# Sorting five of eight batches by expert in a cross-attention and mixture-of-experts kernel

## The chip, the cores and the metric

The kernel runs on one core of a Trainium2 chip. The metric is the device time of one launch in microseconds (us), as the median over runs.

## The reference

The input x is 8 batches of 128 tokens with 256 features, ctx_512 is 8 x 128 x 64. One layer of cross attention (16 heads of 16 features, causal) and one mixture of experts follow each other. The second part is what the change touches:

```python
x = x + xattn(layernorm(x), ctx_512, ...)
xf = layernorm(x)                                    # 1024 tokens x 256
router_logits = xf @ gate_weight.T + xf @ gate_delta.T       # 8 experts
probs = softmax(router_logits)
routing_weights, selected = top_k(probs, 2)
routing_weights = routing_weights / routing_weights.sum(-1, keepdims=True)
gup = einsum('th,eho->teo', xf, gate_up_proj) + lora part    # 256 -> 2 x 128, for every expert
gates, h = split(gup, 2, axis=-1)
h = silu(gates) * h
out = einsum('tei,eih->teh', h, down_proj) + lora part       # 128 -> 256
y = einsum('tkh,tk->th', take_along_axis(out, selected), routing_weights)
x = x + y
```

Each token uses two of the eight experts. The lora parts are folded into the weights once, ahead of the tokens.

## The kernel before

A batch is a tile of 128 tokens. The attention stage goes over the batches one after the other (`for b in range(NT)` on each engine), with scores of batch b + 2, exponentials of b and output projection of b - 2 interleaved. As each batch leaves it, its residual is added, it is normalised (`second_stats` on DVE, `normaliser` on POOL, `x2_normalise` on ACT), transposed (`x2_T` on PE) and split in a high and a low fp32r part (`x2T_high`, `x2T_low`), so that three fast fp32r matmuls stand for one in full precision. The weights are split the same way, `merge_high` on ACT and `merge_lows` on POOL.

The expert stage is dense: every token goes through all eight experts, and a weight that is zero for the six experts not chosen takes them out. Tokens form two groups (NG = 2) of four batches, 512 tokens (GN). The router of a group is `router_logits`, `lg_T`, `route_logits`, `route_choose`, `route_weights`, `w_T`. The weights, transposed to one row per expert, are stored to memory (`w_dram`, L218) and read back as a broadcast to 128 partitions, one 256 KB load for each expert (L226), into `weight_all`, which shares the tile `probsT` with attention. Then 16 steps n follow, 8 experts for each group. A step is on PE `gate_step` and `up_step` (six matmuls each, 512 moving columns, weights stationary, all recorded as L798) and `down_step` (12 matmuls with 256 moving columns, L1087), which sums all experts of a group in two banks; on ACT `silu_step` and `h_high`; on DVE `gate`, `weigh` and `h_low` (L664, L671, L676). PE runs gate_step four steps and up_step three steps ahead of down_step. At a group's end DVE adds the banks to `x_sb` (`add_residual`, L654) and SP stores the result (L231). The order on every engine is written out by hand; semaphores tie them together. In `link` a DVE or POOL instruction is waited for by the next one of its engine.

## Time and profile before

| | |
|---|---|
| median of 3 runs | 170.81 us (170.69 to 171.04) |
| the profiled execution | 170.58 us, its span 168.8 us |
| busy | PE 153.3, DVE 105.4, ACT 80.1, POOL 53.5 us |
| instructions | 3777 |
| granted clock of TensorE, mean | 0.998 |

The span runs from the first to the last instruction; what lies around it is not in the profile. Busy time of an engine is a share of the whole span. PE is matmuls, PEld the loads of their stationary operand, which lie beside matmuls.

### The profile page before, as it was taken

Reading aid. Unit: us, or ns where it says so; the run is one execution under the profiler, and the core shown is the slowest. Engines: PE = TensorE matmul, PEld = TensorE weight load, DVE = VectorE, ACT = ScalarE, POOL = GpSimd, SP = SyncE. Lnnn points to the kernel's source line nnn. Section 1 sums busy time; section 2 is a strip of 40 time slices with the busy share of each in tenths; the row PEclk is TensorE's granted clock in tenths of the full one; section 3 lists DMA queues with packets and bytes.
Section 4 is the critical chain, followed back from the end, with each engine's and each line's share of the span. In section 5 each row is a group of like instructions: output and inputs, shape, how many; then the busy total and the mean of one; then the engine's idle time right before and its main releaser. Section 6 shows DMA issues by size and latency. Waiting matters only on the chain.

```text
span 168.8 us, 3777 instructions
## 1 busy us (share of the span) xinstructions
PE 153.3 (91%) x1481; PEld 118.9 (70%) x1481; DVE 105.4 (62%) x224; ACT 80.1 (47%) x161; POOL 53.5 (32%) x93
## 2 busy tenths in 40 slices
PE   0597999999999999999999997999969989999972
PEld 0365676677777677778778876887758868888961
DVE  2778986859657657835498456555943466444463
ACT  1373557356657776586754617422653022222420
POOL 4276002256378657776740243330000000000000
PEclk9999999999999999999999999999999999999999
DMA  5999940000000000000000185000000594000003
GB/s 148 292 255 229 282 126 2 6 6 0 8 0 8 0 6 2 4 2 4 0 0 4 37 257 209 0 4 0 2 0 4 144 344 137 0 0 0 4 0 124
DMA packets 13042, 11.18 MB, mean 66 GB/s; under 512 B 6457, under 2 KB 10449, under 8 KB 13025
## 3 DMA queue, kind: packets, MB, share of 16 engines
q1 hardware_dynamic: 9584, 7.14, 15.7%
q0 software_dynamic: 544, 2.10, 4.6%
q10 hardware_dynamic: 2896, 1.70, 3.9%
q8 instruction: 12, 0.20, 0.5%
q14 instruction: 6, 0.04, 0.1%
HBM read 9.79 MB, written 1.08 MB: 64 GB/s over the span
## 4 chain that ended last, share of the span: by engine, by line
PE 65%; DVE 14%; DMA 8%; ACT 5%; issue 5%; POOL 1%; DVEq 0%; ACTq 0%
PE bank L798 29%; PE bank L1087 9%; PE bank L908 8%; DMA probsT<-weights 4%; PE bank L894 4%; PE bank L1024 4%; PE bank L915 3%; DVE m_sb L593 2%; DVE h_f L671 2%; DMA x_sb<-in_x 2%; DMA weights<-wT 2%; DVE xhat L552 2%; PE bank L973 2%; ACT silu L410 1%; DVE stats L539 1%
## 5 line engine op out<-in xcount | busy, mean ns | idle before, releaser
L798 PE MATMUL bank<-xT_hi,up_hi 128*128 128x512 f32 x64 | 27.1, 424 | 3.0 <-ACT silu L410 3.0
L318 ACT ACTIVATE h_hi<-h_f 128x512 fp32r<-128x512 f32 x16 | 10.1, 632 | 37.2 <-PE bank L1087 25.9
L295 POOL TENSOR_SCALAR_AFFINE_SELECT probsT<-probsT 128x512 f32<-128x512 f32 x32 | 19.7, 635 | 22.5 <-ACT probsT L391 22.5
L593 DVE TENSOR_REDUCE m_sb<-bank 128x4 f32<-128x512 f32 x32 | 20.4, 685 | 9.4 <-PE bank L908 9.4
L391 ACT ACTIVATE probsT<-bank 128x512 f32<-128x512 f32 x32 | 17.9, 590 | 17.3 <-PE bank L915 17.3
L798 PE MATMUL bank<-xT_hi,up_lo 128*128 128x512 f32 x64 | 25.3, 395 | 0.0
L798 PE MATMUL bank<-xT_lo,up_hi 128*128 128x512 f32 x64 | 25.3, 395 | 0.0
L676 DVE TENSOR_TENSOR h_lo<-h_f,h_hi 128x512 fp32r<-128x512 f32 x16 | 11.4, 713 | 21.0 <-ACT h_hi L318 21.0
L1087 PE MATMUL bank<-dn_hi,h_hi 128*128 128x256 f32 x64 | 18.4, 288 | 1.1 <-DVE h_lo L676 1.0
L915 PE MATMUL bank<-q_f,k_f 32*128 32x128 f32 x256 | 18.6, 283 | 0.0
L798 PEld LDWEIGHTS bank<-xT_hi,up_hi 128*128 128x128 f32 x64 | 12.0, 188 | 8.6 <-ACT silu L410 6.9
L1087 PE MATMUL bank<-dn_hi,h_lo 128*128 128x256 f32 x64 | 17.9, 279 | 0.0
L1087 PE MATMUL bank<-dn_lo,h_hi 128*128 128x256 f32 x64 | 17.8, 279 | 0.0
L908 PEld LDWEIGHTS bank<-k_f,q_f 32*128 32x128 f32 x256 | 13.6, 186 | 5.5 <-issue 5.0
L908 PE MATMUL bank<-k_f,q_f 32*128 32x128 f32 x256 | 16.3, 283 | 0.0
L915 PEld LDWEIGHTS bank<-q_f,k_f 32*128 32x128 f32 x256 | 15.5, 186 | 0.7 <-issue 0.7
L671 DVE TENSOR_TENSOR h_f<-probsT,gated 128x512 f32<-128x512 f32 x16 | 12.0, 748 | 5.1 <-DMA probsT<-weights 4.7
L798 PEld LDWEIGHTS bank<-xT_hi,up_lo 128*128 128x128 f32 x64 | 12.0, 188 | 2.9
L1087 PEld LDWEIGHTS bank<-dn_hi,h_hi 128*128 128x128 f32 x64 | 12.0, 187 | 2.1 <-DVE h_lo L676 1.5
L286 POOL TENSOR_TENSOR up_lo<-up_w,up_hi 128x512 fp32r<-128x512 f32 x8 | 10.3, 1291 | 9.8 <-ACT up_hi L318 9.8
L798 PEld LDWEIGHTS bank<-xT_lo,up_hi 128*128 128x128 f32 x64 | 12.1, 188 | 1.7
L1087 PEld LDWEIGHTS bank<-dn_lo,h_hi 128*128 128x128 f32 x64 | 12.0, 188 | 0.4
(137 smaller groups left out, 284.4 us busy)
## 6 DMA issues: line engine op xcount, KB each, us to landing
probsT<-weights SPq DMA_DIRECT2D x16, 256.0 KB, 5.5
x_sb<-in_x SPq DMA_DIRECT2D x4, 256.0 KB, 4.8
up_w<-in_L_ffn_gate_up_proj ACTq DMA_DIRECT2D x1, 1024.0 KB, 10.4
up_w<-in_L_ffn_gate_up_proj POOLq DMA_DIRECT2D x1, 1024.0 KB, 7.2
dn_w<-in_L_ffn_down_proj POOLq DMA_DIRECT2D x1, 1024.0 KB, 9.3
out<-x_sb SPq DMA_DIRECT2D x4, 256.0 KB, 2.2
ctx_sb<-in_ctx ACTq DMA_DIRECT2D x2, 128.0 KB, 5.6
wq_raw<-in_L_xattn_Wq ACTq DMA_DIRECT2D x1, 256.0 KB, 5.8
```

What stands on the lines that cost most here:

```text
L286: pool.tensor_tensor(merge_slice(up_lo, dn_lo, n), merge_slice(up_w, dn_w, n), merge_slice(up_hi, dn_hi, n).bitcast(F32), ALU.subtract).th ...
L295: pool.affine_select(out=ch, in_=ch, compare_op=ALU.is_ge, fill=0.0, base=0, pattern=[[0, 4], [1, P]], channel_multiplier=-1).then_inc(S_( ...
L318: act.activation(out_, in_, ACT.Copy, scale=scale).then_inc(S_(done), 1)
L391: act.activation(probsT[:, b % 2, 4 * j:4 * j + 4, :].rearrange("p h n -> p (h n)"), bank[2 + j % 2][:, :], ACT.Exp).then_inc(S_("exp_done ...
L593: dve.reduce_max(m_sb[:, b % 2, :].rearrange("p (u j t) -> p j u t", u=2, t=2)[:, c], S_BANK(b, c)[:, :].rearrange("p (u t n) -> p u t n", ...
L671: dve.tensor_tensor(h_f[:, k, :], weight_all[:, n % E, :], gated[:, k, :], ALU.mult).then_inc(S_("h_ready"), 1)
L676: dve.tensor_tensor(h_lo[:, k, :], h_f[:, k, :], h_hi[:, k, :].bitcast(F32), ALU.subtract)\
L798: last = pe.matmul(out_, a, m, start=start and i == 0, stop=stop and i == len(pairs) - 1, **kw)
L894: pe.matmul(S_BANK(s, j)[:, :], ident_b[:, :], causal[:, :, :].rearrange("p h n -> p (h n)"), start=True, stop=True, skip_group_check=True)
L908: last = pe.matmul(S_BANK(s, j)[:, c * P:(c + 1) * P], q_f[rows, c, tokens(s)], k_f[rows, c, tokens(s)], start=False, stop=True, skip_grou ...
L915: last = pe.matmul(bank[2 + j % 2][:, c * P:(c + 1) * P], k_f[rows, c, tokens(t)], q_f[rows, c, tokens(t)], start=True, stop=True)
L1087: last = pe.matmul(bank[6 + t // 2][:, (t % 2) * H:(t % 2 + 1) * H], a[:, k, tok], w[:, e, :], start=i == 0 and t % 2 == 0 and m == 0, sto ...
```

## The change

Batches 0 to 2 (384 tokens, DN) go through the dense stage as before, now in 8 steps. The weights of its router are computed inside the attention loop's last step, and Silu's table is loaded ahead by one activation (`warm`). Batches 3 to 7 (640 tokens) are sorted by expert:

- `choose`, `positions` and `slots` find for each token its two experts and its two row numbers in a buffer `xs` in memory, which has 640 rows for each expert. Ones below the diagonal (`tri`) times the choice counts the tokens ahead within a batch, `ahead` carries the count over batches. This is done for batches 3 and 4, then 5 and 6, then 7.
- POOL scatters every normalised row twice (`scatter_rows`, 10 indirect transfers); a row of 272 elements also carries the number of the row in `ys` where its result belongs. ACT fills xs with a blank before (`fill`).
- `map_tiles` works out which expert and which row of xs each of 17 tiles of 128 rows has. 17 is the most that 1280 rows in 8 groups can need.
- SP reads the row number of each tile into a register and loads the tile. PE reads the weights' column into a register (`pick`) and uses it in nine matmuls: `gate_up_tile` has the tokens stationary and 256 columns of weights moving, `hidden_T` transposes the hidden part, `down_tile` has 256 moving columns.
- POOL scatters the 128 rows of a tile's result into `ys` (`scatter_tile`). When all have landed, SP loads five blocks back (`yg`), DVE (batches 3, 5, 7) and ACT with POOL (4, 6) weigh and add the two rows of each token, and five stores follow.

On DVE the routing stands inside the dense steps: `choose(2)` at n = 0, `choose(3)` and `slots(2)` at n = 1, `slots(3)` and `map_tiles` at n = 2; `choose(1)` and `slots(1)` stand ahead of the loop. ACT and DVE go through the tiles with `silu_tile(n + 1)`, `hT_high(n)`, `x_copy(n + 3)`, `y_copy(n - 1)` and `gate_tile(n + 1)`, `hT_low(n)`, `x_low(n + 3)`, `row_of_y(n)`. `pair_weights` and its Exp come after the last tile. The core of the diff:

```diff
+    DENSE = range(0, 3)
+    SORTED = range(3, NT)
+    DN = len(DENSE) * P
+    NS = len(SORTED)
+    ROWS = NS * P
+    TILES = (2 * ROWS + E * (P - 1)) // P
+    XW = 272
+    BY_DVE = (3, 5, 7)
+    BY_POOL = (4, 6)
+    ROUTED = (tuple(DENSE), (3, 4), (5, 6), (7,))
...
+        xs = nc.dram_tensor("xs", (E * ROWS + P, XW), F32, kind="Internal").ap()
+        ys = nc.dram_tensor("ys", (TILES * P + 2 * ROWS, H), F32, kind="Internal").ap()
+        w_dram = nc.dram_tensor("weights", (E, DN), F32, kind="Internal").ap()
...
+        load_of = lambda n: (0, 1, 1, 2, 2, 2, 3, 3, 3, 3, 4, 4, 4, 4, 5, 5, 5)[n]
...
-            for g in range(NG):
-                sp.wait_ge(S_("wT_copied"), g + 1)
-                sp.dma_start(w_dram[g], wT[:, g, :]).then_inc(S_("w_written"), 16)
-                sp.wait_ge(S_("w_written"), 16 * (g + 1))
-                for i in range(E):
-                    if g == 0:
-                        sp.wait_ge(S_("pv_done"), NT - 1 if i < E // 2 else NT)
-                    else:
-                        sp.wait_ge(S_("h_ready"), i + 1)
-                    e = EXPERTS[i]
-                    sp.dma_start(weight_all[:, i, :], w_dram[g, e:e + 1, :].to_broadcast([P, GN])).then_inc(weight_loaded[i], 16)
...
+            sp.wait_ge(S_("wT_copied"), 1)
+            sp.dma_start(w_dram, wT[:, :]).then_inc(S_("w_written"), 16)
+            sp.wait_ge(S_("w_written"), 16)
+            for i in range(E):
+                sp.wait_ge(S_("pv_done"), NT - 1 if (i + 1) * DN <= NH * P else NT)
+                e = EXPERTS[i]
+                sp.dma_start(weight_all[:, i, :], w_dram[e:e + 1, :].to_broadcast([P, DN])).then_inc(weight_loaded[i // 2], 16)
+            sp.wait_ge(S_("tiles_mapped"), 1)
+            sp.wait_ge(S_("x_scattered"), 16 * 2 * NS)
+            for n in range(TILES):
+                row = sp.value_load(row_x[0:1, n:n + 1], min_val=0, max_val=E * ROWS)
+                sp.dma_start(xt[:, n, :], xs[bass.ds(row, P), :]).then_inc(tile_loaded[load_of(n)], 16)
...
+            sp.wait_ge(S_("y_scattered"), 16 * TILES)
+            for j, b in enumerate(SORTED):
+                sp.dma_start(yg[:, :, j, :], ys[TILES * P:, :].rearrange("(k j p) c -> j p k c", k=2, p=P)[j])\
+                    .then_inc(y_back[(j + 1) // 2], 16)
+            for n, b in enumerate(BY_DVE):
+                sp.wait_ge(S_("pair_added"), n + 1)
+                sp.dma_start(out_v[:, b, :], x_sb[:, b, :]).then_inc(S_("stored"), 16)
+            sp.wait_ge(S_("stored"), 16 * (2 + NS))
...
+            def scatter_rows(t):
+                j = t - SORTED[0]
+                pool.wait_ge(S_("slots_ready"), [t in r for r in ROUTED].index(True))
+                if j == 0:
+                    pool.wait_ge(S_("filled"), 16 * 3)
+                for k, name in enumerate(("x2row_ready", "x2row_again")):
+                    pool.wait_ge(S_(name), j + 1)
+                    pool.indirect_dma_start(xs, bass.IndirectOffsetOnAxis(ap=index[:, k, t:t + 1], axis=0), xrow[:, j, k, :], None,
+                                            bounds_check=E * ROWS - 1).then_inc(S_("x_scattered"), 16)
+            def scatter_tile(n):
+                pool.wait_ge(S_("y_copied"), n + 1)
+                pool.wait_ge(S_("y_row_ready"), n + 1)
+                pool.indirect_dma_start(ys, bass.IndirectOffsetOnAxis(ap=y_row[:, n:n + 1], axis=0), y_at(n),
+                                        None, bounds_check=TILES * P + 2 * ROWS - 1).then_inc(S_("y_scattered"), 16)
...
-            for t in range(NT - 3, NT):
-                normaliser(1, t, t + 1, "mv2_ready", t + 1)
-            merge_lows(4)
+            normaliser(1, 5, 6, "mv2_ready", 6)
+            normaliser(1, 6, 7, "mv2_ready", 7)
+            scatter_rows(3)
+            normaliser(1, 7, 8, "mv2_ready", 8)
+            scatter_rows(4)
+            merge_lows(2)
+            scatter_rows(5)
+            scatter_rows(6)
+            merge_lows(1)
+            scatter_rows(7)
+            merge_lows(1)
+            for n in range(TILES):
+                scatter_tile(n)
+            for n, b in enumerate(BY_POOL):
+                j = b - SORTED[0]
+                for k in range(2):
+                    pool.wait_ge(S_("y_weighed"), 2 * n + k + 1)
+                    ins = pool.tensor_tensor(x_sb[:, b, :], yg[:, k, j, :], x_sb[:, b, :], ALU.add)
+                    if k == 0:
+                        link(ins)
+                    else:
+                        ins.then_inc(S_("pool_added"), 1)
...
+            def fill(lo, hi):
+                act.wait_ge(S_("blank_made"), 1)
+                rows = xs[lo * P:hi * P, :].rearrange("(r p) c -> p r c", p=P)
+                act.dma_start(rows, blank[:, None, :].to_broadcast([P, hi - lo, XW])).then_inc(S_("filled"), 16)
...
+            def x_copy(n):
+                act.wait_ge(S_("xt_T"), n + 1)
...
+                copy(xh_hi[:, n % 3, :, :], XT_BANK(n), "xt_copied")
+            def silu_tile(n):
+                act.wait_ge(S_("gu_ready"), n + 1)
...
+                act.activation(silu_t[:, n % 2, :], bank[2 + n % 2][:, 0:I], ACT.Silu).then_inc(S_("silu_tile"), 1)
+            def hT_high(n):
+                act.wait_ge(S_("hT_ready"), n + 1)
...
+                copy(hT_hi[:, n % 2, :], bank[n % 2][:, 0:P], "hT_high")
+            def y_copy(n):
+                act.wait_ge(S_("tile_down"), n + 1)
+                copy(y_at(n), bank[6 + n % 2][:, 0:H], "y_copied")
...
+            def choose(r):
+                ts = ROUTED[r]
...
+                other = lg[:, lo:hi, None, :].to_broadcast([P, n, E, E])
+                own = lg[:, lo:hi, :, None].to_broadcast([P, n, E, E])
+                fork(dve.tensor_tensor(outranks[:, 0:n, :, 0:E], other, own, ALU.is_gt))
+                link(dve.tensor_tensor(outranks[:, 0:n, :, E:2 * E], other, own, ALU.is_equal))
+                link(dve.tensor_tensor(outranks[:, 0:n, :, E:2 * E], outranks[:, 0:n, :, E:2 * E],
+                                       earlier[:, None, :, :].to_broadcast([P, n, E, E]), ALU.mult))
+                join()
+                link(dve.reduce_sum(rank[:, lo:hi, :], outranks[:, 0:n, :, :], AX.X))
+                link(dve.tensor_scalar(chosen[:, lo:hi, :], rank[:, lo:hi, :], 1.5, None, ALU.is_lt))
...
+            def slots(r):
+                ts = ROUTED[r]
+                lo, hi = ts[0], ts[-1] + 1
...
+                link(dve.tensor_tensor(slot[:, lo:hi, :], slot_at(r, lo, hi).rearrange("p (t e) -> p t e", e=E),
+                                       chosen[:, lo:hi, :], ALU.mult))
+                fork(dve.reduce_max(both[:, 0, lo:hi], slot[:, lo:hi, :], AX.X))
+                link(dve.reduce_sum(slot_sum[:, lo:hi], slot[:, lo:hi, :], AX.X))
+                join()
+                link(dve.tensor_tensor(both[:, 1, lo:hi], slot_sum[:, lo:hi], both[:, 0, lo:hi], ALU.subtract))
+                dve.tensor_scalar(index[:, :, lo:hi], both[:, :, lo:hi], -1.0, None, ALU.add).then_inc(S_("slots_ready"), 1)
+            def map_tiles():
+                n = TILES
+                dve.wait_ge(S_("pos_ready"), len(ROUTED) - 1)
+                link(dve.tensor_tensor(over[:, :, :], count_at[:, :, None].to_broadcast([1, E, NS]), full[:, :, :], ALU.is_gt))
+                link(dve.reduce_sum(n_tiles[:, :], over[:, :, :], AX.X))
+                fork(dve.tensor_scalar(skip[:, :], n_tiles[:, :], -float(P), float(ROWS), ALU.mult, ALU.add))
...
+                link(dve.tensor_scalar(w_at[:, :], n_done[:, :], E - 1.0, float(H), ALU.min, ALU.mult))
+                dve.tensor_scalar(row_x[:, :], row_f[:, :], float(E * ROWS), None, ALU.min).then_inc(S_("tiles_mapped"), 1)
...
+            def x_low(n):
+                dve.wait_ge(S_("xt_copied"), n + 1)
...
+                dve.tensor_tensor(xh_lo[:, n % 3, :, :], XT_BANK(n), xh_hi[:, n % 3, :, :].bitcast(F32), ALU.subtract)\
+                    .then_inc(S_("x_low"), 1)
+            def gate_tile(n):
+                dve.wait_ge(S_("silu_tile"), n + 1)
...
+                dve.tensor_tensor(ht_f[:, n % 2, :], bank[2 + n % 2][:, I:2 * I], silu_t[:, n % 2, :], ALU.mult)\
+                    .then_inc(S_("gated_tile"), 1)
+            def hT_low(n):
+                dve.wait_ge(S_("hT_high"), n + 1)
...
+                dve.tensor_tensor(hT_lo[:, n % 2, :], bank[n % 2][:, 0:P], hT_hi[:, n % 2, :].bitcast(F32), ALU.subtract)\
+                    .then_inc(S_("hT_copied"), 1)
+            def row_of_y(n):
+                dve.wait_ge(tile_loaded[load_of(n)], 16 * loaded_with[n])
+                dve.tensor_tensor(y_row[:, n:n + 1], xt[:, n, H:H + 1].bitcast(I32), dump[:, n:n + 1], ALU.max)\
+                    .then_inc(S_("y_row_ready"), 1)
...
+            def positions(r):
+                pe.wait_ge(S_("chosen_ready"), r)
+                for t in ROUTED[r]:
+                    j = t - SORTED[0]
+                    products(slot_at(r, t, t + 1), [(tri[:, :], chosen[:, t, :]), (ones[:, :], ahead[:, j, :])],
+                             "pos_ready" if t == ROUTED[r][-1] and t != NT - 1 else None)
+                    if t == NT - 1:
+                        products(count_at, [(ones[:, 0:1], ahead[:, j + 1, :])], "pos_ready")
...
+            def tile_T(n):
+                pe.wait_ge(tile_loaded[load_of(n)], 16 * loaded_with[n])
+                if n == 0:
+                    pe.wait_ge(S_("slots_ready"), 2)
+                elif n == 1:
+                    pe.wait_ge(S_("tiles_mapped"), 1)
+                else:
+                    pe.wait_ge(S_("x_low"), n - 1)
+                for ic in range(HC):
+                    last = pe.transpose(XT_BANK(n)[:, ic, :], xt[:, n, ic * P:(ic + 1) * P], ident[:, :])
+                last.then_inc(S_("xt_T"), 1)
+            def pick(n):
+                if n == 0:
+                    pe.wait_ge(S_("tiles_mapped"), 1)
+                columns[n] = pe.value_load(w_at[0:1, n:n + 1], min_val=0, max_val=(E - 1) * H)
+            def gate_up_tile(n):
+                if n < 2:
+                    pe.wait_ge(S_("gated_ready"), E - 1 + n)
+                else:
+                    pe.wait_ge(S_("gated_tile"), n - 1)
+                pe.wait_ge(S_("x_low"), n + 1)
+                picked = lambda w, ic: w[:, ic, :, :].rearrange("p e o -> p (e o)")[:, bass.ds(columns[n], 2 * I)]
+                products(bank[2 + n % 2][:, 0:2 * I],
+                         [(a[:, n % 3, ic, :], picked(w, ic)) for ic in range(HC)
+                          for a, w in ((xh_hi, up_hi), (xh_hi, up_lo), (xh_lo, up_hi))], "gu_ready")
+            def hidden_T(n):
+                pe.wait_ge(S_("gated_tile"), n + 1)
+                if n < 2:
+                    pe.wait_ge(S_("silu_ready"), E - 1 + n)
+                else:
+                    pe.wait_ge(S_("hT_copied"), n - 1)
+                pe.transpose(bank[n % 2][:, 0:P], ht_f[:, n % 2, :], ident[:, :]).then_inc(S_("hT_ready"), 1)
+            def down_tile(n):
+                pe.wait_ge(S_("hT_copied"), n + 1)
+                if n < 2:
+                    pe.wait_ge(S_("out_ready"), n + 1)
+                else:
+                    pe.wait_ge(S_("y_copied"), n - 1)
+                picked = lambda w: w[:, :, :].rearrange("p e h -> p (e h)")[:, bass.ds(columns[n], H)]
+                products(bank[6 + n % 2][:, 0:H], [(a[:, n % 2, :], picked(w)) for a, w in
+                                                   ((hT_hi, dn_hi), (hT_hi, dn_lo), (hT_lo, dn_hi))], "tile_down")
...
-            for n in range(NG * E):
-                if n + 3 < NG * E:
+            for n in range(E):
+                if n + 3 < E:
                     up_step(n + 3)
-                if n + 4 < NG * E:
+                if n == 0:
+                    x2_T(NT - 1)
+                    logits(2)
+                if n == 1:
+                    positions(2)
+                if n + 4 < E:
                     gate_step(n + 4)
-                if n in (0, 1):
-                    x2_T(NT - 2 + n)
+                if n == 0:
+                    logits(3)
                 if n == 2:
-                    router_logits(1, bank[5])
-                if n == 3:
-                    lg_T(1, bank[5])
-                if n == 5:
-                    w_T(1, bank[5])
+                    positions(3)
+                if n >= E - 2:
+                    tile_T(n - (E - 2))
                 down_step(n)
+            for n in range(3):
+                pick(n)
+            gate_up_tile(0)
+            tile_T(2)
+            for n in range(TILES):
+                if n + 1 < TILES:
+                    gate_up_tile(n + 1)
+                if n + 3 < TILES:
+                    tile_T(n + 3)
+                hidden_T(n)
+                if n:
+                    down_tile(n - 1)
+                if n + 3 < TILES:
+                    pick(n + 3)
+            down_tile(TILES - 1)
```

## Rows read from the trace of the kernel before

**Rows 1.** The page: busy time by engine.

```profile
PE 153.3 (91%) x1481; PEld 118.9 (70%) x1481; DVE 105.4 (62%) x224; ACT 80.1 (47%) x161; POOL 53.5 (32%) x93
```

**Rows 2.** Windows: length, busy us of PE, PEld, DVE, ACT, POOL, clock, DMA, GB/s.

```profile
0.00:83.60 83.60, 75.52 (x1022) 55.17 (x1023) 56.78 (x131) 49.60 (x108) 43.27 (x79) 1.00 0.31 70
83.60:101.20 17.60, 17.60 (x115) 14.11 (x113) 12.10 (x33) 7.94 (x15) 6.25 (x12) 1.00 0.22 69
101.20:136.30 35.10, 32.12 (x179) 25.76 (x178) 19.69 (x37) 15.23 (x26) 4.01 (x3) 1.00 0.19 57
136.30:158.20 21.90, 21.88 (x122) 18.32 (x123) 11.50 (x19) 5.59 (x10) 0.00 (x0) 1.00 0.21 73
158.20:168.80 10.60, 6.16 (x48) 5.54 (x47) 5.37 (x9) 1.75 (x3) 0.00 (x0) 0.97 0.15 49
...
20.00:30.00 10.00, 9.85 (x130) 7.01 (x131) 7.70 (x15) 6.26 (x14) 1.22 (x2) 1.00 0.32 90
```

**Rows 3.** Chain of waits: start, duration, what.

```profile
86.64 0.22 PE bank L1005 x2
...
93.88 1.44 DMA weights<-wT
...
95.34 3.55 DMA probsT<-weights
...
142.33 1.41 PE bank L1087 x12
143.74 2.93 PE bank L798 x12
```

**Rows 4.** Timeline of the end of the span: start, duration, engine.

```profile
165.21 0.28 PE L1087 MATMUL bank<-dn_hi,h_lo 128*128 128x256 f32 x1
165.54 1.07 SPq L231 DMA_DIRECT2D out<-x_sb  x2
```

**Rows 5.** Timeline of DVE, 85 to 97 us.

```profile
85.90 0.39 DVE L633 TENSOR_TENSOR above<-lg 128x256 f32<-128x256 f32 x1
86.33 0.43 DVE L634 TENSOR_TENSOR equal<-lg 128x256 f32<-128x256 f32 x1
...
88.72 0.18 DVE L644 TENSOR_TENSOR lpick<-lexp,chosen 128x32 f32<-128x32 f32 x1
88.94 0.19 DVE L645 TENSOR_REDUCE lsum<-lpick 128x4 f32<-128x32 f32 x1
...
95.54 0.42 DVE L615 TENSOR_TENSOR x_sb<-bank,x_sb 128x256 f32<-128x256 f32 x1 [1.81 <-PE bank L798]
```

**Rows 6.** Groups of DVE: operation, shapes, count, busy us, mean ns, idle before.

```profile
L664 DVE TENSOR_TENSOR gated<-bank,silu 128x512 f32<-128x512 f32 x16 | 10.9, 684 | 1.3 <-ACT silu L410 1.3
...
L535 DVE SCALAR_TENSOR_TENSOR xT_lo<-bank,xT_hi 128x256 fp32r<-128x256 f32 x8 | 3.4, 424 | 2.9 <-ACT xT_hi L318 2.8
```

**Rows 7.** Groups of instructions of ACT.

```profile
L318 ACT ACTIVATE o_T<-bank 128x256 f32<-128x256 f32 x8 | 3.0, 380 | 3.4 <-PE bank L984 3.4
...
L410 ACT ACT_TABLE_LOAD x2 | 2.6, 1283 | 0.0
...
L318 ACT ACTIVATE mT<-bank 16x128 f32<-16x128 f32 x8 | 2.0, 251 | 0.8 <-PE bank L938 0.8
```

**Rows 8.** Groups of instructions of POOL.

```profile
L286 POOL TENSOR_TENSOR up_lo<-up_w,up_hi 128x512 fp32r<-128x512 f32 x8 | 10.3, 1291 | 9.8 <-ACT up_hi L318 9.8
...
L270 POOL DMA_DIRECT2D up_w<-in_L_ffn_gate_up_proj x1 | 1.1, 1110 | 0.0
L273 POOL DMA_DIRECT2D dn_w<-in_L_ffn_down_proj x1 | 0.9, 932 | 0.0
```

**Rows 9.** Timeline of SP's queue, 93 to 103 us.

```profile
95.34 4.38 SPq L226 DMA_DIRECT2D probsT<-weights  x8
```

**Rows 10.** Issues of DMA: count, KB each, median us to landing.

```profile
probsT<-weights SPq DMA_DIRECT2D x16, 256.0 KB, 5.5
...
out<-x_sb SPq DMA_DIRECT2D x4, 256.0 KB, 2.2
```

564 lines of the change are left out of this document (370 added, 194 removed).

## The prediction, made before the kernel ran

> **What bounds the kernel now.** I read the page first. PE is busy for 91% of the span, far ahead of DVE, ACT and POOL [rows 1]. Next the table of windows: the attention stage ends near 83.6 us, and from there to the last matmul PE leaves little open (17.60 of 17.60, 32.12 of 35.10, 21.88 of 21.90 us), at the full clock of 2.4 GHz (1.00) [rows 2]. So the second half is a queue of matmuls, and only fewer matmul columns can shorten it much. The chain of waits then gives the unit of that half: one expert step of a group of 512 tokens takes 2.93 us for 12 matmuls of gate and up and 1.41 us for 12 of down, 4.34 us together, and there are 16 such steps, 69.4 us [rows 3]. The same chain shows where PE waited: the routing weights go out to memory (1.44 us) and come back to all partitions (3.55 us) [rows 3], and the same once more for the second group, near 130 us. Last, the end: the last matmul runs from 165.21 to 165.49 us, and an addition and a store follow, 3.3 us to the end of the span [rows 4].
>
> **The change part by part, on PE.** A matmul over 512 moving columns costs 2.93/12 = 0.244 us, one over 256 costs 1.41/12 = 0.118 us [rows 3]. Halfway between them, 384 columns are 0.181 us. The dense stage with three batches: 12 x 0.181 + 9 x 0.118 = 3.23 us a step, 8 steps 25.8 us. A sorted tile has the tokens stationary and 256 weight columns moving: 6 x 0.118 + 3 x 0.118 = 1.06 us. Its three transposes cost 0.11 us each, since a pair takes 0.22 [rows 3]: 0.33 us. That is 1.39 us a tile and 23.6 us for 17. Expert work on PE falls from 69.4 to 49.4 us: 20.0 us taken off the engine that sets the end. The sorting is paid for by latency: routing before, a trip through memory before, and one behind.
>
> **When the dense stage ends.** The first expert matmul stays near 83.6 us. In the window 83.60:101.20 before, PE did nine half steps (9 x 1.47 = 13.2 us), which leaves 4.4 us for other things (values, output projections, transposes) [rows 2]; I count 6 us for these with the small matmuls of logits, positions and later transposes. PE alone would end the dense stage at 83.6 + 6 + 25.8 = 115.4 us. But DVE has to route in the middle of it. A small DVE instruction with its link to the next costs 0.22 us, a larger one 0.45 us [rows 5]. From these, choosing for batches 5 and 6 is about 2.2 us, for batch 7 1.6, two times slots 2.2, the map of tiles (13 instructions) 2.9: 8.9 us, all within the first three expert steps. Gate, weigh and low part of a step are 3 x 0.57 = 1.7 us at 384 columns (0.69 at 512, 0.42 at 256) [rows 5, 6]. So these three steps take DVE 3 x 1.7 + 8.9 = 14.0 us where PE needs 9.7, and each down step waits for its low part. DVE enters them near 96 us, as the last batch's residual was added at 95.54 [rows 5], and leaves them at 110. Behind that lie three half steps (3 x 1.09), five down steps (5 x 1.06), two transposes of tiles (0.4) and some 1.5 us of waits on gate and low part: 120.5 us, 5 us behind what PE alone could do. Two things come back: the weights of the dense batches are chosen while attention still runs, so the first trip (93.88 to 98.89 us) starts about 7 us earlier, as soon as values(7) frees its tile, and the second trip, with the switch to Exp and back (1.28 us each) [rows 7], is gone. Both are in the sum, as it counts no bubbles of their kind.
>
> **When the first tile can start.** Slots of batch 7 are ready near 108.5 us by that count. POOL has then two scatters of 5, two of 6, a merge of 1.29 us [rows 8] and two of 7. No indirect scatter is in this trace; nearest is POOL's own issue of a plain DMA, 0.93 to 1.11 us [rows 8]. The price may be as low as the 0.55 us of an issue on SP or as high as the 2.2 us in which a store lands [rows 9, 10]; I take 1.1, because it is the same engine. Then all rows are in memory near 116 us, and tile 0, with one load behind it, is there at about 118.5 us. Tiles 1 and 2 follow by 121. I put the first sorted matmul at 122.5 us, 2 us behind the dense stage: three picks in a row stand in front of it on PE, and only one down step can lie over them. I add 1.0 us for the group of tiles 3 to 5: SP issues one load in 0.55 us (eight in 4.38) [rows 9] and must also read a row number first, so 17 loads take some 20 us, slower at the start than the tiles are wanted.
>
> **The loop of 17 tiles.** ACT has two operations of 128 columns (0.25 us each, after mT) and two of 256 (0.38 each) [rows 7]: 1.26 us. DVE has 0.42 + 2 x 0.30 + 0.18 = 1.20 us [rows 5, 6]. POOL has one scatter, 1.1 us. SP has about 1.2 us. All are under PE's 1.39, and every tile is buffered at least twice, so no handoff closes a circle within a tile. What the trace cannot price is the register: one read on PE's queue for each tile (pick) and nine matmuls whose weights it names. Bounds: nothing, since PE's queue runs ahead while matmuls are pending; 0.55 us, the nearest instruction that a sequencer handles by itself, when nothing hides it. pick stands behind down_tile(n - 1), whose three matmuls (0.35 us) lie over it, and what is queued behind it is the next gate_up_tile, for which ACT and DVE then wait. I take 0.16 us exposed, 1.55 us a tile: 26.4 us. The two ends are 23.6 and 33.0 us.
>
> The Trainium skill (DMA: Bandwidth & Descriptors, section Latency and other measured facts) puts a floor of about 600 ns under a tensor_load, the read of a register. No run here shows one yet. By that rule, an estimate with all of it exposed, a tile would take 1.99 us and the whole would be 171.8 us.
>
> **The tail.** Behind the last down matmul: copy of y 0.4; its scatter on POOL 1.1; landing in memory 2.2, as a store to out; five loads issued on SP at 0.55, 2.7; the last one lands 3.0 later (the first broadcast took 3.55, the median of sixteen queued ones was 5.5) [rows 3, 9, 10]; two additions 0.8; store 2.2: 12.4 us, against 3.3 before [rows 4]. The pair weights and the load of Exp's table (1.28 us, about 3 us together) lie beside the scatter and the loads. Bounds: 9 us if issues and landings overlap, 17 us if the loads take the 5.5 us and the scatter 2.2.
>
> **Other edits** cost nothing that shows. The added constants on POOL, some twenty operations of 0.1 to 0.5 us, come behind the load of dn_w, beside a POOL that is busy 1.22 us of the ten from 20 to 30 us [rows 2]; if they delay the first mask they cost up to 3 us. The fill of the 41 blocks of xs on ACT's queue is three issues of 0.55 us [rows 9] in the attention stage, where ACT is busy 49.60 of 83.60 us [rows 2].
>
> **The sum.** 122.5 + 1.0 + 26.4 + 12.4 = 162.3 us of span against 168.8. The profiled execution took 170.58 us, 1.8 us outside its span, and the median of the runs is 0.2 above it: 164.3 us, 3.8% faster than 170.81.
>
> **Rivals.** *PE's queue becomes the bound.* The register read and the nine matmuls with a computed address take more of PE's queue than the matmuls hide. For it: nine of twelve matmuls of a tile are affected, and the wait in front of down_tile leaves the queue little lead: the high and low copies of a tile's hidden part come 0.25 + 0.30 us and some 0.2 of handoffs behind its transpose, the down step one tile time (1.39) behind it, so about 0.6 us. Against it: matmul pairs go out every 0.118 us now with nothing visible between them. It decides from 0.38 us more a tile (6.5/17), at 1.93 us; 0.55 us exposed gives 170.9, and with 0.03 us more for each of the nine matmuls, 2.2 us a tile, 175.4 us, slower. *The scatters on POOL set the loop.* At 2.2 us each the loop takes 37 us and the scatters of x another 4 us late: 179 us; at 1.6 us it is hardly seen. For it, only that this trace has no scatter. *The sorted stage starts late.* Routing, scatter and loads are one chain through five engines; if first tiles come 6 us later, PE idles, the clock may be taken down (0.97 in the last window, where PE was busy 6.16 of 10.6 us [rows 2]), and the time is 170 us, no change. *Everything overlaps.* DVE catches up, the first sorted matmul is at 118.5 us, a tile takes 1.40 us and the tail 10 us: 118.5 + 0.5 + 23.8 + 10 + 2 = 154.8 us.
>
> **Chances.** The forecast, with a tile at 1.4 to 1.85 us and the stage ends 3 us to either side: 0.52, own range 158 to 170. Everything overlaps 0.10. Late start 0.13, split evenly about no change (0.05, 0.03, 0.05). PE's queue 0.18, nearly all slower (0.01 no change). Scatters 0.07. Faster 0.52 + 0.10 + 0.05 = 0.67, within 0.2% (about what a measurement of this kernel can tell from no change) 0.04, slower 0.29. The range runs from the overlapping case to the slow queue, 156 to 175 us; beyond lie half of the overlapping case, most of the scatters and the worst of the queue.
>
> **What the profile after would show.** Dense gate matmuls at 0.18 us, the first tile matmul near 122.5 us, tiles every 1.55 us, the last down matmul near 150 us, then 12 us of copy, scatter, load and store. In the chain of waits the loop should be PE's. If it shows issue on PE between down_tile and gate_up_tile, the queue is the bound; if y_scattered comes long after the last copy, POOL is. A hole on PE ahead of the first tile means that routing is late. Most likely wrong are the price of a register-named tile and the 5 us that PE loses to routing on DVE.

## The result and the profile after

The changed kernel takes 183.37 us, median of 4 runs (181.49 to 187.41), beside 170.93 (170.69 to 171.39) for the kernel before on the same chip: a ratio of 1.061, 95% interval 1.056 to 1.066. It is slower by 6.1%; 164.3 us were predicted. Ratios here and below rest on the executions within 1.5% of the kernel's fastest, and two of these four lie above that, with a lower clock (185.09 and 187.41 us). Its profiled execution took 181.49 us, its span 179.7 us, where the sum of the prediction gave 162.3.

The page's first row, to be held against [rows 1]:

```profile
PE 143.6 (80%) x1493; PEld 116.1 (65%) x1493; DVE 115.8 (64%) x311; ACT 90.0 (50%) x220; POOL 86.5 (48%) x141
```

The 20 us of matmuls that the change takes away are not to be seen: busy PE fell from 153.3 to 143.6 us. The windows say why, and where the time is (attention stage, then the stretch to the first sorted tile, the tiles, the tail; columns as in [rows 2]):

```profile
0.00:83.60 83.60, 75.95 (x1025) 55.85 (x1026) 57.16 (x132) 48.65 (x107) 45.77 (x95) 1.00 0.47 138
83.60:101.20 17.60, 15.49 (x124) 13.83 (x122) 12.36 (x38) 9.38 (x21) 7.05 (x13) 1.00 0.34 105
101.20:131.40 30.20, 24.33 (x145) 22.07 (x145) 24.40 (x60) 10.13 (x22) 13.71 (x14) 0.89 0.19 63
131.40:163.20 31.80, 27.86 (x200) 24.38 (x200) 17.52 (x70) 18.20 (x66) 14.38 (x15) 1.00 0.40 124
163.20:179.70 16.50, 0.00 (x0) 0.00 (x0) 4.42 (x12) 3.66 (x7) 5.61 (x7) 0.58 0.44 144
```

From 101.2 to 131.4 us DVE and PE are busy alike (24.4 and 24.3 us of 30.2), neither of them full, and the mean clock is 0.89: it stands at 1.2 GHz from 104.5 to 107.9 and from 121.6 to 125.0 us. The last dense matmul ends at 130.50 us, where the prediction had 120.5, and the first sorted one comes at 131.46 us, 9 us behind the 122.5 of the prediction.

The chain of waits through the start of that stage and its third and fourth tiles (start, duration, what):

```profile
127.00 1.96 DMA xt<-xs
129.00 0.44 PE bank L1426 x2
129.44 1.06 PE bank L1408 x9
130.50 0.96 issue
131.46 0.97 PE bank L1096 x6
...
135.84 0.97 PE bank L1096 x6
136.81 0.22 PE bank L1426 x2
137.03 0.11 PE bank L1451
137.13 0.35 PE bank L1096 x3
137.49 0.18 issue
137.67 1.02 PE bank L1096 x6
```

First PE waits for a tile from memory, then 0.96 us for nothing that the profile shows; those are the three picks. From there a tile takes 1.82 to 1.96 us, but for one of 2.22 (135.84 to 137.67 is 1.83), of which 1.39 are matmuls and transposes as priced. The reads of a register on PE's queue, from the view of that line (minimum/median/maximum ns, first and last start):

```profile
L1432 PEldq TENSOR_LOAD <-w_at x17: 297/302/706, 129.1 to 157.7; - x17
L1432 PEldq FUSED_REGOPS  x17: 146/151/165, 129.6 to 158.1; - x17
L1432 PEldq SEQ_ASSERT  x17: 18/18/28, 129.8 to 158.3; - x17
```

Four rows of DVE's timeline and four of POOL's in the dense stage:

```profile
104.58 2.76 DVE L838 TENSOR_TENSOR outranks<-lg 128x128 f32<-128x128 f32 x1
107.26 0.28 DVE L839 TENSOR_TENSOR outranks<-lg 128x128 f32<-128x128 f32 x1
...
117.67 1.99 DVE L893 TENSOR_SCALAR row_x<-row_f 1x17 int32<-1x17 f32 x1
...
121.77 2.25 DVE L970 TENSOR_TENSOR h_lo<-h_f,h_hi 128x384 fp32r<-128x384 f32 x1 [0.59 <-ACT h_hi L449]
```
```profile
104.67 1.28 POOL L382 TENSOR_TENSOR dn_lo<-dn_w,dn_hi 128x512 fp32r<-128x512 f32 x1
105.90 1.27 POOL L382 TENSOR_TENSOR up_lo<-up_w,up_hi 128x512 fp32r<-128x512 f32 x1
...
118.34 1.28 POOL L382 TENSOR_TENSOR dn_lo<-dn_w,dn_hi 128x512 fp32r<-128x512 f32 x1
...
122.31 1.29 POOL L382 TENSOR_TENSOR dn_lo<-dn_w,dn_hi 128x512 fp32r<-128x512 f32 x1
```

An instruction of 0.28 us took 2.76, one of 0.17 took 1.99, one of 0.56 took 2.25: 6.0 us more, and each ends within 0.5 us of the end of POOL's additions. By the profile `row_x`, begun at 117.67 us, is late before the addition begins at 118.34, while an indirect scatter still runs on POOL; e4 decides between the two.

The tail, in the chain of waits:

```profile
163.78 0.98 POOL ys L399
164.76 0.30 issue
165.06 2.42 DMA ys<-xt,y_row
...
168.43 4.32 DMA probsT<-ys
...
172.83 0.52 ACT probsT L712
...
173.42 1.01 POOL x_sb L439
...
174.50 0.61 POOL x_sb L439
...
175.25 0.90 POOL x_sb L439
```

The last down matmul ends at 163.11 us and the span at 179.7: 16.6 us, for which 12.4 were predicted. POOL starts the last scatter 1.5 us after its data are there, a load lands after 4.32 us, and two batches are added on POOL.

### The profile page after: what moved, and what is told of

The parts are those of the page before. It is cut to its first block, busy times and chain, and to the rows that moved or that the text cites. A ratio compares the mean times of both kernels' runs of the same rounds, so it can differ in the third digit from the quotient of the medians.

```text
span 179.7 us, 4442 instructions
## 1 busy us (share of the span) xinstructions
PE 143.6 (80%) x1493; PEld 116.1 (65%) x1493; DVE 115.8 (64%) x311; ACT 90.0 (50%) x220; POOL 86.5 (48%) x141
## 3 DMA queue, kind: packets, MB, share of 16 engines
q10 hardware_dynamic: 8480, 7.68, 13.3%
## 4 chain that ended last, share of the span: by engine, by line
PE 49%; DVE 16%; issue 11%; POOL 9%; DMA 8%; ACT 2%; SPq 2%; POOLq 1%; DVEq 0%; ACTq 0%
PE bank L1096 22%; PE bank L1206 7%; PE bank L1192 4%; POOL xs L393 3%; PE bank L1332 3%; PE bank L1213 3%; DMA probsT<-ys 2%; DVE m_sb L795 2%; PE bank L1426 2%; POOL ys L399 2%; DMA x_sb<-in_x 2%; DVE outranks L838 2%; DVE xhat L754 2%; POOL x_sb L439 1%; DMA xs<-xrow,index 1%
## 5 line engine op out<-in xcount | busy, mean ns | idle before, releaser
L399 POOL DMA_INDIRECT ys<-xt,y_row x17 | 16.6, 977 | 25.8 <-DVE y_row L948 24.4
L1206 PE MATMUL bank<-k_f,q_f 32*128 32x128 f32 x256 | 16.3, 283 | 0.0
L393 POOL DMA_INDIRECT xs<-xrow,index x10 | 10.4, 1039 | 10.0 <-DVE index L874 7.5
L1096 PE MATMUL bank<-up_hi,xh_hi 128*128 x34 | 11.2, 328 | 4.3 <-DVE ht_f L936 2.2
L1096 PE MATMUL bank<-xT_hi,up_hi 128*128 128x384 f32 x32 | 12.2, 380 | 2.0 <-DVE gated L958 2.0
L578 ACT ACTIVATE silu_t<-bank 128x128 f32<-128x128 f32 x17 | 4.7, 278 | 13.5 <-PE bank L1096 12.2
L1096 PE MATMUL bank<-xT_hi,up_lo 128*128 128x384 f32 x32 | 11.1, 348 | 0.0
L1096 PEld LDWEIGHTS bank<-up_hi,xh_hi 128*128 128x128 f32 x34 | 6.4, 187 | 7.3 <-issue 7.3
L1096 PE MATMUL bank<-xT_lo,up_hi 128*128 128x384 f32 x32 | 10.9, 341 | 0.0
L1192 PE MATMUL bank<-causal,ident_b 128*128 128x512 bf16 x32 | 9.6, 380 | 1.2 <-DVE q_f L766 0.5
L1096 PE MATMUL bank<-up_lo,xh_hi 128*128 x34 | 9.6, 284 | 0.0
L1096 PE MATMUL bank<-up_hi,xh_lo 128*128 x34 | 9.5, 280 | 0.0
```

Source lines behind the costliest of these rows:

```text
L393: pool.indirect_dma_start(xs, bass.IndirectOffsetOnAxis(ap=index[:, k, t:t + 1], axis=0), xrow[:, j, k, :], None, bounds_check=E * ROWS - ...
L399: pool.indirect_dma_start(ys, bass.IndirectOffsetOnAxis(ap=y_row[:, n:n + 1], axis=0), y_at(n), None, bounds_check=TILES * P + 2 * ROWS - ...
L1096: last = pe.matmul(out_, a, m, start=start and i == 0, stop=stop and i == len(pairs) - 1, **kw)
L1192: pe.matmul(S_BANK(s, j)[:, :], ident_b[:, :], causal[:, :, :].rearrange("p h n -> p (h n)"), start=True, stop=True, skip_group_check=True)
L1206: last = pe.matmul(S_BANK(s, j)[:, c * P:(c + 1) * P], q_f[rows, c, tokens(s)], k_f[rows, c, tokens(s)], start=False, stop=True, skip_grou ...
```

## The experiments

Each profile is cut at the same three points: the first dense matmul (86.05 us in the changed kernel), the first tile matmul, the start of the last down matmul. "Low" is the time at 1.2 GHz before the tail, and behind it how much of that lies between the first dense and the first tile matmul. All in us; the median has the fastest execution beside it. The kernel before had medians of 170.8 to 171.4 us beside them.

| kernel | median (fastest) | first dense | to first tile | tiles | tail | low (in "to first tile") |
|---|---|---|---|---|---|---|
| prediction | 164.3 | 83.6 | 38.9 | 27.4 | 12.4 | 0 |
| changed | 183.37 (181.49) | 86.05 | 45.4 | 31.4 | 16.9 | 6.8 (6.8) |
| e1 | 184.62 (182.83) | 87.80 | 46.6 | 31.7 | 17.8 | 17.1 (12.5) |
| e2 | 182.84 (180.75) | 89.21 | 45.5 | 30.3 | 17.3 | 14.3 (6.8) |
| e3 | 182.59 (180.84) | 86.24 | 45.2 | 31.6 | 16.6 | 3.4 (3.4) |
| e4 | 183.25 (181.44) | 88.36 | 44.9 | 31.5 | 16.6 | 13.7 (6.8) |
| e5 | 183.27 (182.24) | 90.23 | 49.8 | 26.0 | 16.3 | 23.9 (12.2) |
| e6 | 183.69 (182.31) | 90.92 | 46.5 | 32.4 | 14.6 | 23.9 (8.9) |
| e7 | 180.01 (176.66) | 88.84 | 41.0 | 31.5 | 16.2 | 10.2 (4.0) |
| e8 | 179.03 (174.58) | 90.61 | 46.8 | 25.9 | 14.7 | 23.9 (12.6) |
| e9 | 175.72 (173.94) | 88.42 | 39.4 | 31.3 | 14.9 | 6.8 (3.4) |
| e10 | 174.02 (173.44) | 86.30 | 39.4 | 31.5 | 15.0 | 6.8 (3.4) |
| e11 | 174.59 (173.49) | 85.93 | 40.3 | 31.3 | 14.8 | 6.8 (6.8) |
| e12 | 173.88 (173.32) | 86.23 | 39.3 | 31.5 | 15.0 | 3.4 (3.4) |
| e13 | 170.97 (170.37) | 86.64 | 39.3 | 28.1 | 14.9 | 3.4 (3.4) |
| e14 | 168.20 (167.57) | 86.25 | 40.6 | 24.9 | 15.1 | 6.8 (6.8) |
| e15 | 168.26 (167.78) | 86.06 | 40.5 | 24.8 | 15.1 | 6.8 (6.8) |
| e16 | 178.14 (177.63) | 90.34 | 45.7 | 25.5 | 16.7 | 17.1 (8.6) |

The clock falls for 3.4 or 6.8 us at a time; the expectations below, read from coarser windows, say 3.5 and 7.5. What 3.4 us more of it cost can be read from e11, e14 and e15 beside e9, e12 and e13: 0.9 to 1.2 us to the first tile (e14 and e15 also differ in their reads).

**e1: the pick earlier in the tile.**

```diff
                 if n + 1 < TILES:
                     gate_up_tile(n + 1)
                 if n + 3 < TILES:
+                    pick(n + 3)
                     tile_T(n + 3)
...
-                if n + 3 < TILES:
-                    pick(n + 3)
```

> PE's pick of tile n+3 stands directly behind gate_up_tile(n+1), ahead of tile_T(n+3), instead of behind down_tile(n-1). The loop of the changed kernel takes 1.83 to 1.90 us a tile where the matmuls and transposes of a tile take about 1.4. Theory A (the register read is an exposed latency in front of the next gate_up_tile): with the transposes and the down step queued behind the read, about 0.35 us a tile comes back for 14 tiles, a tile takes 1.45 to 1.55 us, and the time falls by 4 to 5 us, to 178 or less. Theory B (PE's queue needs as long for the read and its nine register-named matmuls as PE does for the tile, wherever they stand): the period stays at 1.8 to 1.9 us and the time is that of the changed kernel within 0.5 us.

The period stayed at 1.81 to 1.98 us, but for one of 2.19; the hole moved from in front of gate_up_tile to in front of tile_T. Theory A falls: the read is not a latency that work queued behind it can cover.

**e2: no register** (the experts' order is left out, the tiles go through fixed columns).

```diff
-                columns[n] = pe.value_load(w_at[0:1, n:n + 1], min_val=0, max_val=(E - 1) * H)
+                columns[n] = n * E // TILES * H
```

> No register at all: the weights of tile n stand at a constant column, so that which expert a tile goes through is left out (the amount of work is the same). This bounds what the register costs in all. Theory A and theory B both: a tile takes 1.39 to 1.5 us, and the time falls by 5 to 8 us (three reads in front of the first tile, 0.96 us, and 0.35 to 0.45 us for each of 14 tiles). If the tile still takes 1.8 us or more, the register is not what stretches it, and the handoffs between PE, ACT and DVE are.

Where tiles follow each other undisturbed they take 1.40 us (142.73, 144.13, 145.53, 146.93). The whole loop is only 1.1 us shorter, as PE now waits for the tiles: SP needs 1.09 us for the read and the issue of each. The size of the register's price, 0.45 us a tile, is clear; that the time did not fall by 5 to 8 us was a miss. Waits for loads take part of it; the low clock (14.3 us) may take another, which no run separates.

**e3: the normaliser first.**

```diff
-            scatter_rows(3)
             normaliser(1, 7, 8, "mv2_ready", 8)
+            scatter_rows(3)
```

> On POOL the normaliser of batch 7 stands ahead of the scatter of batch 3's rows instead of behind it. In the changed kernel mv2 of batch 7 was ready at 98.49 us, the normaliser ran from 100.50 to 101.75 us behind that scatter, and PE stood from 100.24 to 102.44 us. Theory A (that place alone makes the hole): the hole and the low clock after it go, routing of batch 7 comes 2 us earlier, and the time falls by 2 to 3 us. Theory B (DVE is what is late in the dense stage, and the hole only moves): less than 0.5 us.

The hole shrank from 2.20 to 0.80 us and the low clock behind it went, and PE then waited 1.26 and 3.05 us for DVE further on; the tiles began at 131.45 us, as before. That is theory B.

**e4: the additions of weight halves moved ahead.** The last four halves are copied on ACT beside copy_weights, and:

```diff
+            merge_lows(2)
             normaliser(1, 5, 6, "mv2_ready", 6)
+            merge_lows(2)
             normaliser(1, 6, 7, "mv2_ready", 7)
             scatter_rows(3)
             normaliser(1, 7, 8, "mv2_ready", 8)
             scatter_rows(4)
-            merge_lows(2)
             scatter_rows(5)
             scatter_rows(6)
-            merge_lows(1)
             scatter_rows(7)
-            merge_lows(1)
```

> POOL's last four additions of expert weight halves (merge_lows, about 1.27 us each) and their first halves on ACT are moved ahead, so that none stands between scatters. In the changed kernel three DVE instructions took 2.76, 1.99 and 2.25 us where their like take 0.28, 0.17 and 0.56, about 6 us more in all, and each ended with such an addition on POOL. Theory A (the additions on POOL hold DVE up): no DVE instruction of the dense stage takes over 1.2 us, the tiles start 4 to 7 us earlier, and the time falls by 4 to 7 us. Theory B (POOL's indirect scatters hold DVE up): instructions of 2 us and more on DVE remain beside the scatters, and the time changes by less than 1.5 us, as POOL's additions were not in the way of the scatters by more than that.

The cause was right and its worth wrong. From 88 to 130 us no DVE instruction takes over 0.56 us now, with the same scatters running beside them, so the additions held DVE up and the scatters did not. The other runs agree: the seven profiles that keep additions among the scatters (the changed kernel, e1 to e3, e5, e6, e16) each have three DVE instructions of 2.0 to 3.5 us in this stage, the ten other changed kernels none over 0.8 us (86 to 131 us). But the tiles start only 0.5 us earlier, counted from the first dense matmul. The rows of DVE and POOL in e4 show what took its place:

```profile
108.40 0.36 DVE L846 TENSOR_TENSOR ahead<-ahead,chosen 128x8 bf16<-128x8 bf16 x2
111.91 0.56 DVE L968 TENSOR_TENSOR h_lo<-h_f,h_hi 128x384 fp32r<-128x384 f32 x1 [3.15 <-ACT h_hi L448]
...
115.58 0.17 DVE L872 TENSOR_SCALAR index<-both 128x4 uint32<-128x4 f32 x1
```
```profile
116.56 0.97 POOL L393 DMA_INDIRECT xs<-xrow,index  x1 [9.61 <-DVE index L872]
117.84 0.98 POOL L393 DMA_INDIRECT xs<-xrow,index  x1 [0.30 <-issue]
```

Batches 5 and 6 are chosen at 108.8 us; then DVE stands for 3.15 us in front of an h_low, with choose(3) and slots(2) written behind it, and POOL waits 9.61 us for the index and then has six scatters in a row. The h_hi that DVE waits for waits in turn for PE's first down step, which stands on PE behind a hole of 2.21 us (to 104.75, for the normaliser of batch 7) and in a stretch at 1.2 GHz (105.4 to 112.3 us): its matmuls start 0.213 us apart, those of the next down step 0.118. So part of the 3.15 us is clock and part is order.

**e5: all picks ahead of the loop.**

```diff
+            PICKS = ((), (), (), (), range(0, 3), range(3, 7), range(7, 12), range(12, TILES))
...
+                for m in PICKS[n]:
+                    pick(m)
                 if n >= E - 2:
                     tile_T(n - (E - 2))
                 down_step(n)
```

> All 17 picks stand ahead of the down steps 4 to 7 of the dense stage (3, 4, 5 and 5 of them), where PE waits for DVE and for the first tiles anyway; none is left in the loop. Each takes PE's queue about 0.5 us (TENSOR_LOAD 0.30, FUSED_REGOPS 0.15, SEQ_ASSERT 0.02). Theory B, refined (the queue is full in the loop, and one register read more is 0.45 us more per tile, wherever it stands in the loop): a tile takes 1.40 to 1.50 us, the loop is about 6 us shorter, the dense stage 3 to 5 us longer than it was, so the time falls by 1 to 4 us. Rival (the nine register-named matmuls are the dear part): the period stays above 1.7 us and the time rises by 3 us or more.

From the sixth on every tile takes 1.39 to 1.40 us, with the same register-named matmuls: they cost nothing more, the read costs all. But PE stood 2.09 and 2.07 us in front of tiles 0 and 1, with five reads in front of each: over 0.4 us a read in the dense stage too. What the loop gave, the dense stage took, with a share for the clock (12.2 us low in that stretch, 6.8 in the changed kernel).

**e6: the tail.**

```diff
-    BY_DVE = (3, 5, 7)
-    BY_POOL = (4, 6)
+    BY_DVE = (3, 4, 5, 6, 7)
+    BY_POOL = ()
...
-            for j, b in enumerate(SORTED):
+            for j in (0, 2, 4):
                 sp.dma_start(yg[:, :, j, :], ...).then_inc(y_back[j], 16)
...
+            for j in (1, 3):
+                act.dma_start(yg[:, :, j, :], ...).then_inc(y_back[j], 16)
```

> Only the tail differs from the changed kernel: the reads of y come back on two queues (three on SP, two on ACT) with a semaphore each, and DVE adds all five batches, POOL and ACT none. In the changed kernel the five reads took SP 2.43 us to issue, and four additions on POOL (0.6 to 1.0 us each, 3.54 together) ended at 176.96 us where DVE was done at 175.6. Expected: from the last down matmul to the end of the span 13.5 to 14.5 us instead of 16.6, so 2 to 3 us less. If the transfers themselves are the limit, less than 1 us.

The tail is 2.3 us shorter, as expected. The time is not, and this kernel's clock was low for 24 us, against 7.

**e7: the order of routing**, with the moves of e3 and e4.

```diff
# PE
-                if n == 1:
-                    positions(2)
+                if n == 1:
+                    positions(3)
...
                     logits(3)
-                if n == 2:
-                    positions(3)
+                    positions(2)
# DVE
                 if n == 0:
                     choose(2)
-                if n == 1:
                     choose(3)
                     slots(2)
-                if n == 2:
+                if n == 1:
                     slots(3)
                     map_tiles()
```

> Three changes of order, nothing else: normaliser 7 ahead of the scatter of batch 3, the last additions of weight halves moved ahead, and choose(3), slots(2), slots(3) and map_tiles each one expert step earlier on DVE, with their positions on PE. In the run with the additions moved, DVE stood idle from 108.8 to 111.9 us with batches 5 and 6 chosen, their index came at 115.8, and six scatters in a row (1.28 us each) ended at 123.9. Theory (the order of routing, not its amount, makes the tiles late): the last row lands 3 to 5 us earlier, PE no longer waits for tile 0, the stage of tiles starts 3 to 5 us earlier from the first dense matmul, and the time falls by 3 to 5 us. Rival (PE's own work and its three picks end then anyway): less than 1.5 us.

The first tile comes 4.4 us earlier behind the first dense matmul (41.0 for 45.4 us) and PE no longer waits for it. Two things besides the order bear on the 4.4 us. The clock was low for 4.0 us of the stretch instead of 6.8, about 1 us by what e11, e14 and e15 show. And e7 holds the moves of e3 and e4 too, which alone gave 0.2 and 0.5 us; the two together without the new order were not run. So the order is the likeliest cause of some 3 us, and its share alone is not shown.

**e8: e5, e6 and e7 together.**

> The picks ahead, the new tail and the new order of routing together. If the three act on different stretches their gains add: 2 + 2.5 + 4 = 8 to 10 us below the changed kernel, 172 to 175 us, still not faster than the kernel before. With the granted clock whole (it falls to 1.2 GHz for 3.5 or 7.5 us at a time, at one to three places, in the runs so far) it would be near 170.

The gains of e6 and e7 are there, those of e5 again given back in front of the tiles; the clock was low for 24 us.

**e9 to e12: TensorE's clock.** e9 is e7 with the tail of e6 and only three picks in the dense stage. e10 spreads the fill of xs, e11 widens the router, e12 does both.

```diff
# e10, e12
-                if b in (0, 2, 4):
-                    fill(7 * b, min(7 * b + 14, E * NS + 1))
+                if b < 7:
+                    fill(6 * b, min(6 * b + 6, E * NS + 1))
# e11, e12
+                        out_ = bank[1][:, tokens(t)].rearrange("p (r e) -> p r e", e=E)
-                        products(out_, [(xt[:, ic, tokens(t)], w[:, ic, :]) for ic in range(HC)
+                        products(out_, [(xt[:, ic, tokens(t)], w[:, ic, None, :].to_broadcast([P, P // E, E])) for ic in range(HC)
```

> The new order of routing and the new tail together, with the picks in the loop, but the first three ahead of the down steps 5 to 7 of the dense stage. The order of routing alone gave 180.0 us, the tail took 14.3 us in place of 16.6. Expected: 176.5 to 178.5 us. It is the base for the next three runs, whose subject is TensorE's granted clock. In the runs so far it fell to 1.2 GHz behind a hole of 0.86 to 1.28 us on PE near 38 us (five of nine profiles) and near 82 to 93 us with no hole at all (seven of nine), for 3.5 to 7.5 us each; in the kernel before it never did.

> The base, with the fill of xs issued as seven transfers of 6 blocks over batches 0 to 6 instead of three of 14. Theory (the hole near 38 us, in which PE waits for nothing that the profile shows, is PE's instruction fetch held up behind 1.9 MB of fill): the hole is under 0.3 us, the clock does not fall near 40 us, and the time is 1 to 3 us less than the base where the base shows the hole. Rival (the hole has nothing to do with the fill): it stays at 0.9 us and the time is the base's.

> The base, with the 18 router matmuls of the dense batches moving 128 columns (the router's 8, repeated 16 times; the result is read from the first 8) instead of 8. They run from 79 to 81 us, one every 0.11 us, and take as long with 128 columns (0.118 us for 256 in the dense stage). Theory (the clock falls near 82 to 93 us because PE moves few columns in the 2 us before): it does not fall there, the first dense matmul comes 1.5 to 3.5 us earlier, and the time is 1.5 to 3.5 us less than the base. Rival (nothing to do with the router): the base's time and clock.

> The base with the fill spread and the wide router. If both theories hold, the attention stage runs at the full clock as in the kernel before, the first dense matmul stands at 84 to 86 us, and the time is 172 to 175 us; still slower than the kernel before (171), by what is left: 0.45 us for the register read in each of 14 tiles, a tail of 14 us in place of 3, and a dense stage of 40 us in which the clock falls once.

(The hole near 38 us is in six of those nine profiles, not five, and the clock fell behind it in four.) The ratios to the kernel before are 1.023 (1.016 to 1.029) for e9, 1.020 (1.014 to 1.025) for e10, 1.020 (1.013 to 1.026) for e11, 1.017 (1.013 to 1.020) for e12: all still slower, and too near each other to say what either edit is worth in time. The row of PE in e9, and the windows of e10 and e12 over the router's end:

```profile
39.55 0.37 PE L1220 MATMUL bank<-q_f,k_f 32*128 32x128 f32 x1 [0.95 <-issue]
```
```profile
80.00:85.00 5.00, 5.00 (x40) 3.92 (x40) 3.57 (x12) 3.08 (x7) 3.24 (x7) 0.76 0.02 7
```
```profile
80.00:85.00 5.00, 4.83 (x47) 3.94 (x46) 3.29 (x11) 2.85 (x7) 3.24 (x8) 1.00 0.03 10
```

The clock first. With the narrow router it fell between 81.5 and 93 us in ten of twelve profiles (all but those of the changed kernel and of e3); with the wide one in none of five (e11 to e15). In the row of e10 PE is busy for 5.00 of 5.00 us and the clock is 0.76 all the same: ahead of the fall the two kernels differ in the columns of the router's matmuls, not in how busy PE is. The kernel before agrees. Its router moves 512 columns at this place, and its clock does not fall. The changed kernel and e3 keep their clock with the narrow router, so that it makes a fall likely, not certain. A router matmul before, then in e10:

```profile
78.80 0.50 PE L798 MATMUL bank<-xT_hi,wr_hi 128*128 128x512 f32 x1
```
```profile
79.05 0.25 PE L1103 MATMUL bank<-wr_hi,xT_lo 128*128 128x8 f32 x1
```

Then the hole. With the fill in three parts it is in eight of twelve profiles (e1, e2, e5 to e9, e16), with the fill spread in none of five (e10, e12 to e15). Why four with three parts escape (the changed kernel, e3, e4, e11) can be read from the queue of instructions. The DMA queues from 30 to 36 us, in the changed kernel (no hole), then in e9 (hole):

```profile
q10 hardware_dynamic: 1384, 1.51, 72.9%
q8 instruction: 1, 0.02, 1.1%
```
```profile
q10 hardware_dynamic: 1194, 1.30, 61.3%
```

q10 carries the fill, q8 brings instructions in packets of 16,384 bytes. The four that escape have a packet on q8 at 30.6 to 31.7 us, as the fill begins. In all eight with the hole it comes only at 36.3 to 37.3 us, and PE resumes 1.3 to 1.6 us after it is in. With the fill spread it comes at 31.7 (e14) or at 34.3 to 35.0 us, still without a hole. So the instructions come late behind the fill, and that is the hole; that q8 is PE's queue is inferred from this agreement alone.

**e13 to e16: what of a read is dear.** One instruction reads PICK columns, without the check of their bounds: 1 in e13, 4 in e14, 17 in e15, all on e12, and 17 on the changed kernel alone in e16.

```diff
+                if n % PICK:
+                    return
...
-                columns[n] = pe.value_load(w_at[0:1, n:n + 1], min_val=0, max_val=(E - 1) * H)
+                hi = min(n + PICK, TILES)
+                _, values = nc.values_load_multi_w_load_instructions(
+                    w_at[0:1, n:hi], engines=[mybir.EngineType.PE], min_val=0, max_val=(E - 1) * H,
+                    skip_runtime_bounds_check_because="map_tiles writes multiples of H below E * H")
+                columns.update(zip(range(n, hi), values))
```

> The kernel with fill spread and wide router, whose reads of a tile's column leave out the check of its bounds (FUSED_REGOPS 0.15 us and SEQ_ASSERT 0.02 us behind each TENSOR_LOAD of 0.30 us). If the cost is queue time, instruction by instruction, a tile takes 1.65 to 1.72 us in place of 1.86 and the time is 2 to 2.5 us less, 171.5. If the cost is the round trip of the read alone, a tile stays at 1.8 us or more.

> As e13, but one TENSOR_LOAD reads the columns of four tiles into four registers. If its time is mostly the round trip (0.30 to 0.4 us for four), three of four tiles take 1.40 us and each fourth 1.7 to 1.8: 14 tiles give back 5 us against the kernel with 17 single reads, 168.5 to 169.5 us, faster than the kernel before. If each register costs as much as a read, the gain is that of e13.

> As e13, but one TENSOR_LOAD in the dense stage reads all 17 columns. If a further register costs under 0.05 us, all tiles take 1.40 us: 6 us less than with single reads, 167.5 to 168.5 us. If it costs 0.2 us a register, that is 3.5 us in front of the dense stage's sixth down step and the gain is 2 to 3 us only.

> The changed kernel with nothing else changed but its picks: one TENSOR_LOAD of 17 registers, without the bounds check, in front of gate_up_tile(0). A tile takes 1.40 us, 14 of them give back 6 us; the hole of 0.96 us in front of the first tile stays between 0.3 and 1 us. So 176 to 178 us: the register alone does not make the change pay, since 9 us of late start and 4 us of tail stay.

The reads of e14, then of e15, on PE's queue:

```profile
L1447 PEldq TENSOR_LOAD <-w_at x5: 316/343/524, 119.5 to 146.9; - x5
```
```profile
L1447 PEldq TENSOR_LOAD <-w_at x1: 1550/1550/1550, 119.2 to 119.2; - x1
```

Without the check a tile takes 1.53 to 1.90 us, 1.65 in the mean over twelve (128.20 to 148.00): the cost is queue time, instruction by instruction. Four registers at once cost 0.34 us where one costs 0.30, seventeen 1.55, and from the fourth on all tiles, those with a read too, take 1.39 to 1.49, better than the 1.7 to 1.8 expected. e13 stands at a ratio of 1.000 (0.997 to 1.002) to the kernel before, e15 at 0.983 (0.977 to 0.990), and e14, level with it, has 168.20 us, ratio 0.982 (0.976 to 0.987). e16 shows the register alone: 178.14 us, 1.040 (1.034 to 1.045).

## Why the prediction was wrong

By its own terms: the first sorted matmul 9.0 us late, the tiles and the 1.0 us in front of them 4.2 us longer, the tail 4.2 us. 162.3 + 9.0 + 4.2 + 4.2 = 179.7.

- **The work on PE** was right: 0.175 us a matmul of 384 columns (0.181 said), a tile of 1.39 us, seen bare as 1.40 in e5, e14 and e15.
- **"When the dense stage ends"** is the step that failed. It counted DVE's work, 14.0 us for three expert steps from 96 to 110 us, as if it ran without a gap. DVE ended the map of tiles at 119.7 us. The index of batch 7 was ready at 115.0 us for 108.5, all rows were in memory at 123.7 for 116, and tile 0 was there at 126.8 for 118.5. The count left out two things. One is POOL's additions (6.0 us more on DVE), which the trace before shows too, though in it they held up only two instructions of this stage; one of them took 1.52 us for its usual 0.68 (DVE, then POOL):

```profile
110.65 1.52 DVE L671 TENSOR_TENSOR h_f<-probsT,gated 128x512 f32<-128x512 f32 x1
110.34 1.29 POOL L286 TENSOR_TENSOR dn_lo<-dn_w,dn_hi 128x512 fp32r<-128x512 f32 x1 [0.87 <-ACT dn_hi L318]
```

The other is what is queued behind a waiting h_low: DVE has one order, and in it stand the index of the sorted batches and the low parts of the dense ones, which wait for ACT and through it for PE. e4 took the 6.0 us away and such a wait took their place; e7 changed the order as well, and 4.4 us came back, about 1 us of them clock.
- **"The first expert matmul stays near 83.6 us"** was 2.45 us off: PE waited 1.15 us for the dense weights, chosen in front of the stage. In the other profiles with the narrow router it came as late as 90.9 us, with the hole near 38 us and up to 11.5 us of low clock ahead of it. No term of the sum stood for TensorE's clock, since the trace before shows it whole to the last window [rows 2].
- **The scatters** cost 0.98 us and 0.30 between two of them, 1.28 for the 1.1 taken. From the index of batch 7 to its last row in memory it took 8.75 us for the 7.5 of the sum; a small part of the lateness, and e7 has the same ten scatters.
- **The three picks** in front of the first tile were named, with 2 us between the dense stage and the first sorted matmul; 0.96 us showed.
- **The register in the loop** was mis-sized: 0.16 us a tile said, 0.45 measured, 14 x 0.29 = 4.1 us. The reason for the low value, that down_tile's matmuls lie over the read, is the one that e1 refuted. The rival of PE's queue was right in kind but below its point (1.93 us), and wrong in its second half: the matmuls named by a register cost nothing more (e5). The Trainium skill's floor of about 600 ns (DMA: Bandwidth & Descriptors, section Latency and other measured facts) gave 1.99 us a tile; this trace reads 0.30 us for the TENSOR_LOAD and about 0.5 with what follows it (in e5, where reads follow each other, most start 0.63 to 0.68 us apart), so the measurement decides, though the rule was nearer than my value.
- **The tail** was 12.4 us in the sum and 16.6 in the trace: POOL started the last scatter 1.5 us late behind its earlier ones, and it landed 2.4 us after its start, where 3.3 were counted; from there to the last read landed it took 6.7 us for 5.7, from there to the last addition on POOL 2.8 for 0.8, and from there to the end 2.7 for 2.2. That is 1.5 - 0.9 + 1.0 + 2.0 + 0.5 = 4.1 us. Reads on two queues and all additions on DVE gave 2.3 us back (e6).
- **The rivals.** "The sorted stage starts late" was right in mechanism, with its low clock, at 9 us rather than 6; the register and the tail came on top of it. The prediction let only one thing go wrong at a time: late start, queue and tail together were in none of its cases, and that is why 183 us lies outside its range.

So the saving of 20 us on PE holds by the price of its matmuls, and was spent. Before, the last down matmul ended at 165.5 us; less 20 that is 145.5, and it ended at 163.1: 14 x 0.45 = 6.3 us on PE's queue in the tiles, and the remaining 11.3 us are waits, low clock and picks, mostly ahead of them. With 13.3 us more of tail that is 10.9 us more of span. With the order of routing, the router's width, the fill, the tail and the reads mended it pays 1.8%.

## What to carry to other kernels

When work is made to depend on data, cost the chain that makes the data in the order in which each engine holds it: ask of every wait what is queued behind it on its engine, for DVE and POOL as for PE. A register read belongs to the queue's time, not to latency; read several values with one instruction and leave out a bounds check that the data make needless. Once a change makes holes, count the clock: PE can be busy in every microsecond, with matmuls of few columns, and its clock still fall.

## What the runs showed of the hardware

- Some of DVE's instructions on operands in SBUF are held up while POOL adds two tiles from SBUF: 0.28 us became 2.76 beside two additions of 1.28. Not all are: beside the addition at 88.54 us in e4, a DVE addition with one operand in PSUM took 0.41 us and a statistics instruction on one tile its usual 0.43. That agrees with the Trainium skill (SBUF — State Buffer, section SBUF: two separate sides), which says that DVE, in some modes or with two inputs in SBUF, and GpSimd lock a port pair in turn, each for a whole instruction. The held `row_x` instruction reads one tile only, and no run shows which case it is. POOL's indirect scatters beside DVE cost it next to nothing (e4).
- A read of one register on PE's queue takes 0.30 us, of four 0.34, of seventeen 1.55; the bounds arithmetic and its assertion 0.17. Where reads with both follow each other, most start 0.63 to 0.68 us apart (e5). On SP a read and an issue take 1.09 us together.
- TensorE's clock fell to 1.2 GHz for 3.4 or 6.8 us at a time: behind holes of 2 us, behind five of the eight holes of 0.86 to 1.28 us near 38 us, and behind 18 matmuls of 8 columns in a row without a hole. The same matmuls with 128 columns took as long and kept the clock.
- PE stood 0.86 to 1.28 us for no event near 38 us in eight of the twelve profiles that write 1.9 MB to memory in one transfer there. The Trainium skill (Runtime: NRT & Kernel Launch, section Instruction fetch mechanics) says that instructions come in blocks of 16 KiB by a DMA queue of their own; the page of the changed kernel agrees with 13 packets and 0.21 MB on such a queue. In the eight, a block that the other four have at 30.6 to 31.7 us came at 36.3 to 37.3 us, behind most of the fill, and PE went on 1.3 to 1.6 us after it.
- In e4 ACT began a copy (h_hi, at 125.11 us) 2.4 us after everything that it waits for by the profile was done; no run explains that.
